# Second attention with float32 scores, each head in its own 32 rows of the array

## The chip, the cores and the metric

The kernel runs on one core of one Trainium2 chip. The metric is the device time of one execution in microseconds. The core's engines are named as in the profile: PE (TensorE, matmuls), PEld (its weight loads), DVE (VectorE), ACT (ScalarE), POOL (GpSimd) and SP, whose queue issues DMA transfers.

## What is computed

Eight sequences of 512 tokens with 128 features go through four residual steps. This case is about the third, a causal attention with 16 heads of 8 features and rotary position encoding:

```python
def _L1_attn_ref(x, W_qkv, W_out):        # x is layer-normed before
    qkv = jnp.einsum('bti,oi->bto', x, W_qkv)
    qkv = qkv.reshape(Bsz, Tlen, 3 * NUM_HEADS, HEAD_DIM).transpose(0, 2, 1, 3)
    q, k, v = jnp.split(qkv, 3, axis=1)
    q = _apply_rope(q, cos_sin); k = _apply_rope(k, cos_sin)
    scores = jnp.einsum('bhqd,bhkd->bhqk', q, k) / np.sqrt(HEAD_DIM).astype(np.float32)
    scores = jnp.where(causal[None, None], scores, -jnp.inf)
    attn = jax.nn.softmax(scores, axis=-1)
    o = jnp.einsum('bhqk,bhkd->bhqd', attn, v)
    o = o.transpose(0, 2, 1, 3).reshape(Bsz, Tlen, D_MODEL)
    return jnp.einsum('bti,oi->bto', o, W_out)

x = x + _L0_attn_ref(...)   # first attention: windowed, dilated and global
x = x + _L0_ffn_ref(...)    # mixture of experts
x = x + _L1_attn_ref(_layernorm(x, axis=-1), L1_attn_W_qkv, L1_attn_W_out)
x = x + _L1_ffn_ref(...)    # second mixture, two rounds
```

## The kernel before

The four steps run one after the other. Both attentions are one function, `attention` (line 35), called with `causal` false for the first (tiles named w...) and true for the second (tiles named c...). X, the residual, stays in SBUF.

The second attention has 32 slots: 8 sequences (b) by 4 groups (g) of 4 heads; slot n is b = n // 4, g = n % 4. One hand-written order of events, built by `slot` and `chain` and walked by every engine in `walk`, sets the order on each engine; semaphores tie the engines together. A slot has 8 units (i = 0 to 7). In unit i of slot n PE issues one matmul for maxima, the scores of the unit, a second matmul for maxima, and then the events put at i. The maxima belong to slots ahead: those of slot n + 1 in units 0 and 1, those of slot n + 2 in units 2 to 7.

- **Operands of the scores.** q and k are each split into three bfloat16 parts (`part1`, `left1`, `part2`, `left2`, on ACT and POOL, for the first sequence on DVE), written to DRAM (`parts_out`, line 787) and read back stacked into `QS` and `KS`, 72 rows of products a head (`stacks`, lines 798 and 802), with rows 96 to 98 for the maxima. `stacks` issues 6 DMAs a group, `parts_out` 6 a sequence.
- **Maxima** (`smax`, line 393): for each of 4 heads and 4 query blocks t one matmul, queries on the output partitions, (t + 1) x 128 keys as columns, into one of two buffers of the PSUM tile `SM`. DVE adds the mask and reduces it to one column of `NM` (line 622), after which the buffer is free. `maxima_parts` (lines 661 and 665) splits the 16 columns into three bfloat16 parts, PE turns them (`rows`, line 400), DVE copies the 12 rows (line 673) and SP writes them into `QS` with 3 DMAs (line 810).
- **Scores** (`scores`, line 417): unit i takes head i % 4 and two key blocks, 512 and 384 queries in units 0 to 3, 256 and 128 in units 4 to 7, into one of two buffers of `ST`; ACT takes the Exp (line 543), POOL zeroes above the diagonal (line 772).
- **Values**: `pv` (line 463) is float32 with 32 columns a head, so that four heads stand side by side in the array's columns, at unit 6 (first half) and unit 2 of the next slot (second half); `evac` (line 550) evicts it on ACT at unit 3, `sel` (line 472) turns the result at unit 5.
- **Once a sequence**: normalisation, `xT`, `proj` and `rot` (lines 369 and 375, q or k times cosine and a turned copy times sine, line 585, added in `join`), `values`, `vcopy`, `heads_T`, `out_proj`. `xT`, `values`, `rows`, `sel`, `heads_T` and `out_proj` share the PSUM bank `MI` in turn; `proj` and `rot` borrow halves of `ST` (`lend`).

POOL's queue also holds the gathers of the mixture's results into X (lines 711 and 719). SP's queue holds all the DMAs of the stage in program order.

Of the kernel before, what the change touches and what calls it, by code (L numbers as in the profile page):

```python
# [25 lines left out]
MR0 = 96  # L26

# [7 lines left out]
def attention(nc, X, const, w, scratch, causal, due=None):  # L35
# [19 lines left out]
    with nc.cleanup_on_exit(), ExitStack() as ctx:  # L55
# [6 lines left out]
        QS = sb("qs", [P, H, S], BF16)  # L62
        KS = sb("ks", [P, H, S], BF16)
        ML = sb("ml", [SPLIT, 2, 2 * HG, S], BF16)
# [9 lines left out]
        QK = sb("qk", [P, 2, S])  # L74
        QR = sb("qr", [P, 2, S])
        PT = sb("pt", [P, 2, SPLIT, S], BF16)
        TQ = sb("tq", [P, 2, S])
        M = sb("m", [P, HG, NT, NT * DIL])
        MD = sb("md", [P, HG, NT, NT * DIL])
        NM = sb("nm", [P, KINDS * HG, NT])  # L80
        NR = sb("nr", [P, KINDS * HG, NT])
        MT = sb("mt", [P, NT, MROWS], BF16)
        MR = sb("mr", [MROWS, S], BF16)
        OS = sb("os", [P, 2, S])
        JUNK = sb("junk", [P, 4, S], BF16) if causal else None
# [16 lines left out]
        s_pr = sem("pr")  # L102
# [23 lines left out]
        MRD = SPLIT if causal else 2 * SPLIT  # L126
        NNO = 2 if causal else 3
        NV = 1 if causal else 2
        NPT = 3 if causal else 2
# [7 lines left out]
        def second(g, at, put):  # L137

            for i in list(at):
                at[i] = [e for e in at[i] if not (e[1] == 1 and e[0] in ("part1", "left1", "part2", "left2", "parts_out"))]  # L140
            if g == 0:
                for t in range(NT):
                    put(2 * t + 1, "results", 2, t, 1)

        def slot(n):
# [13 lines left out]
            if causal:  # L159
                put(3, "evac", n - 1)  # L160
                put(CUT - 1, "maxima", n + 1)
                put(CUT + 1, "rows", n + 1)
                put(5, "sel", n - 1)
                if g == 0:
                    put(-1, "stacks", b, 3)
                    put(1, "part1", b + 1, 1)
                    put(3, "left1", b + 1, 1)
                    put(4, "vcopy", b, 2)
                    put(5, "part2", b + 1, 1)
                    put(6, "left2", b + 1, 1)  # L170
                    put(7, "parts_out", b + 1, 1)
# [7 lines left out]
                if g == 2:  # L179
# [3 lines left out]
                    put(4, "proj", b + 2, 0)  # L183
                    put(5, "rot", b + 2, 0)
                    put(7, "join", b + 2, 0)
                if g == 3:
                    put(0, "stacks", b + 1, 2)
                    put(1, "part1", b + 2, 0)
                    put(3, "left1", b + 2, 0)
                    put(4, "proj", b + 2, 1)  # L190
                    put(4, "vcopy", b + 1, 0)
                    put(4, "vcopy", b + 1, 1)
                    put(5, "part2", b + 2, 0)
                    put(5, "rot", b + 2, 1)
                    put(6, "left2", b + 2, 0)
                    put(7, "parts_out", b + 2, 0)
# [1897 lines left out]
```

## Time and profile before

| | us |
|---|---|
| median of 3 runs | 2036.46 (2025.91 to 2037.03) |
| the profiled execution | 2029.46 |
| its span, first to last instruction | 2027.8 |
| mean granted TensorE clock | 0.898 |
| PE busy in the span | 1630.1 (80%) |
| DVE busy | 1157.7 (57%) |
| ACT busy | 883.5 (44%) |
| POOL busy | 616.0 (30%) |

### The profile page before, as it was taken

To read this page: it belongs to the slowest core of one execution; us is meant where nothing else is said; L and a number is where in the kernel's file an instruction comes from. 1 tells how busy PE (TensorE), PEld (TensorE's weight loads), DVE (VectorE), ACT (ScalarE), POOL (GpSimd) and SP (SyncE) were. 2 spreads that over 40 slices of the span, in tenths; PEclk is the share of its full clock that TensorE was granted. 3 is DMA by queue.
4 is the path that set the end of the run, shared out by engine and by line. 5 is a ranking of instruction groups with operands and counts; after the bars stand their busy time and mean duration, and the time that the engine had idled before them with its cause. 6 is when DMAs were issued, how large, how long until landed. Compare 5 with 4: busy or idle time off the path is not lost. (4 is left out here: it accounts for less than half of the span.)

```text
span 2027.8 us, 35597 instructions
## 1 busy us (share of the span) xinstructions
PE 1630.1 (80%) x11387; PEld 888.1 (44%) x11489; DVE 1157.7 (57%) x3354; ACT 883.5 (44%) x1406; POOL 616.0 (30%) x879
## 2 busy tenths in 40 slices
PE   1899999999999999579899994468888888616683
PEld 1244444444444443355566663124444444514563
DVE  4756676656667664226333333468888877344584
ACT  1255555656565655431133331045555555402242
POOL 1001010101010100003522223376666533454467
PEclk8699999999999999679999997589999999557897
DMA  3110101111111100322011111233333220235442
GB/s 104 37 52 23 45 22 46 28 42 35 42 39 29 42 26 3 125 42 43 9 40 43 43 43 27 61 69 75 75 75 74 68 64 27 82 121 148 128 115 58
DMA packets 92786, 115.08 MB, mean 57 GB/s; under 512 B 13977, under 2 KB 76223, under 8 KB 92350
## 3 DMA queue, kind: packets, MB, share of 16 engines
q1 hardware_dynamic: 75710, 91.10, 16.5%
q0 software_dynamic: 16896, 21.69, 4.6%
q8 instruction: 99, 1.62, 0.3%
q14 instruction: 81, 0.66, 0.1%
HBM read 73.93 MB, written 39.34 MB: 56 GB/s over the span
## 5 line engine op out<-in xcount | busy, mean ns | idle before, releaser
L543 ACT ACTIVATE we<-wst 128x1024 f32<-128x1024 f32 x384 | 386.1, 1025 | 303.4 <-PE wst L430 158.8
L625 DVE TENSOR_REDUCE wm<-wsm 128x16 f32<-128x512 f32 x512 | 335.7, 685 | 259.5 <-PE wsm L393 255.6
L622 DVE CUSTOM_DVE_ANT_0 cjunk<-csm,const 128x128 bf16<-128x128 f32 (+3 forms) x512 | 232.5, 486 | 78.9 <-PE csm L393 70.3
L543 ACT ACTIVATE ce<-cst 128x896 f32<-128x896 f32 (+1 forms) x256 | 179.2, 704 | 186.0 <-PE cst L417 184.6
L393 PE MATMUL wsm<-wks,wqs 96*128 96x512 bf16 x512 | 191.3, 398 | 32.8 <-DMA wks<-qk_parts 20.2
L393 PE MATMUL csm<-cks,cqs 96*128 96x128 bf16 (+3 forms) x512 | 157.8, 315 | 69.1 <-DVE cnm L622 43.1
L772 POOL TENSOR_SCALAR_AFFINE_SELECT ce<-ce 128x256 f32<-128x256 f32 x256 | 125.3, 506 | 160.0 <-ACT ce L543 159.2
L434 PE MATMUL wst<-wqs,wks 128*128 128x512 bf16 x442 | 139.2, 385 | 9.5 <-issue 5.3
L1606 DVE TENSOR_TENSOR abhh<-absg,abup 128x512 f32<-128x512 f32 x72 | 49.5, 688 | 152.5 <-ACT absg L1585 152.5
L463 PE MATMUL woa<-we,wv 128*32 128x512 f32 x1024 | 132.0, 636 | 1.6 <-ACT we L543 1.6
L393 PEld LDWEIGHTS csm<-cks,cqs 96*128 96x128 bf16 x512 | 51.1, 100 | 182.6 <-DVE cnm L622 117.3
L1622 POOL DMA_INDIRECT abxb<-rows,asource x72 | 68.2, 947 | 162.3 <-DVE abys L1613 145.6
L417 PE MATMUL cst<-cqs,cks 128*128 128x384 bf16 (+3 forms) x480 | 106.6, 299 | 5.0 <-ACT ce L543 1.3
L422 PE MATMUL wst<-wml,const_b 3*128 3x512 bf16 x256 | 100.1, 391 | 9.3 <-ACT we L543 9.3
L430 PE MATMUL wst<-wqs,wks 96*128 96x128 bf16 x1024 | 105.9, 227 | 0.0
L1585 ACT ACTIVATE absg<-abup 128x512 f32<-128x512 f32 x72 | 43.0, 597 | 140.4 <-PE abup L1554 140.4
L393 PEld LDWEIGHTS wsm<-wks,wqs 96*128 96x128 bf16 x512 | 47.6, 98 | 122.5 <-DVE wm L625 61.0
L463 PE MATMUL coa<-ce,cv 128*32 128x512 f32 (+3 forms) x1024 | 92.3, 482 | 8.5 <-POOL ce L772 8.5
L430 PEld LDWEIGHTS wst<-wqs,wks 96*128 96x128 bf16 x1024 | 63.0, 108 | 60.1 <-issue 60.1
L761 POOL COPY wv<-wvs 128x128 f32<-128x128 f32 x32 | 9.3, 290 | 228.4 <-ACT wvs L503 200.2
L1554 PE MATMUL abup<-awg,abxt 128*128 x144 | 75.1, 604 | 2.3 <-ACT abxt L1591 2.3
L1574 PE MATMUL aby<-awd,abht 128*128 x576 | 76.2, 276 | 0.1
(318 smaller groups left out, 2987.7 us busy)
## 6 DMA issues: line engine op xcount, KB each, us to landing
wqs<-qk_parts SPq DMA_DIRECT2D x96, 96.0 KB
wks<-qk_parts SPq DMA_DIRECT2D x96, 96.0 KB
cqs<-qk_parts SPq DMA_DIRECT2D x96, 96.0 KB
cks<-qk_parts SPq DMA_DIRECT2D x96, 96.0 KB
b1r<-rows SPq DMA_DIRECT2D x40, 194.0 KB, 2.6
qk_parts<-wpt SPq DMA_DIRECT2D x48, 128.0 KB, 2.4
qk_parts<-cpt SPq DMA_DIRECT2D x48, 128.0 KB, 2.4
b0r<-rows SPq DMA_DIRECT2D x40, 130.0 KB, 2.5
```

The source lines that it names most:

```text
L393: pe.matmul(SM[:, j % 2, 0:keys], QS[0:MR0, h, t * P:(t + 1) * P], KS[0:MR0, h, 0:keys], start=True, stop=True, skip_group_check=True).the ...
L417: m = pe.matmul(st[:, at:at + width], KS[:, h, kb * P:(kb + 1) * P], QS[:, h, kb * P:S], start=True, stop=True, skip_group_check=True)
L422: pe.matmul(st[:, at:at + S], const["ones_b"][0:SPLIT, :], ML[:, g % 2, kind * HG + hs, :], start=True, stop=False, skip_group_check=True)
L430: m = pe.matmul(out, k, q, start=False, stop=(t == NT - 1), skip_group_check=True)
L434: m = pe.matmul(st[:, c * S:(c + 1) * S], KS[:, h, kb * P:(kb + 1) * P], QS[:, h, :], start=True, stop=True)
L463: m = pe.matmul(OA[VW * hs:VW * (hs + 1), S - width:S], V[:, kb, g * HG + hs, 0:VW], E[:, e_slot(g, HG * r + hs), at:at + width], start=(c ...
L543: act.activation(E[:, e_slot(g, i), 0:width], ST[:, (U * g + i) % 2, 0:width], ACT.Exp, scale=SCALE).then_inc(s_ex, 1)
L622: dve.tensor_tensor_reduce(JUNK[:, j % 4, 0:keys], SM[:, j % 2, 0:keys], const["mask_wide"][:, S - keys:S], 1.0, -3e38, ALU.add, ALU.max, ...
L625: dve.tensor_reduce(M[:, hs, t, :].rearrange("p (w f) -> p w f", f=DIL), SM[:, j % 2, :].rearrange("p (w i f) -> p w f i", w=NT, f=DIL), A ...
L772: pool.affine_select(e, e, [[0, 2], [1, P]], ALU.is_ge, 0.0, base=0, channel_multiplier=-1).then_inc(s_tri, 1)
L1554: m = pe.matmul(UP[:, i % 2, w, 0:F], XT[:, i % 2, :], weight[:, bass.ds(e * F, F)], start=True, stop=True)
L1574: m = pe.matmul(Y[:, j % 2, 0:D], HT[:, j % 2, c * P:(c + 1) * P], WD[:, bass.ds(e * HB * D + c * D, D)], start=(c == 0), stop=(c == HB - 1))
```

## The change

In the second attention only (`causal` true):

- q and k are not split. They stay float32 in the tile `QK`, now with two sequences' room, and 12 DMAs a group copy each head's 8 rows from there into the first 8 of the head's own 32 partitions, of `QM` (queries for the maxima), `KS` and `QS`. Nothing goes through DRAM; `part1`, `left1`, `part2`, `left2`, `parts_out` are gone.
- Maxima and scores are float32 matmuls over a head's 32 partitions (`lanes`). The maxima go by decreasing t, heads in the order 2, 3, 0, 1, so that the heads of a unit's maxima and scores all differ.
- A score unit is one key block and two heads, in the two banks of an `ST` buffer: 512 queries in units 0 and 1, 384 in 2 and 3, 256 in 4 and 5, 128 in 6 and 7.
- `maxima_parts` is gone: PE turns `NM` itself (float32), ACT and no longer DVE copies 4 rows, and SP writes each head's row by itself, 4 DMAs.
- `turned` takes the place of `proj` and `rot`: half of the tokens at a time, `qkv` and `rot` side by side in one bank (`MI` from the third sequence on, no longer `ST`), multiplied by a constant that holds cosines and sines side by side. It stands at other units, and `stacks` of group 0 at unit 0 in place of 3.

```diff
@@ slot
-                put(CUT - 1, "maxima", n + 1)
                 put(CUT + 1, "rows", n + 1)
                 put(5, "sel", n - 1)
                 if g == 0:
                     put(-1, "stacks", b, 3)
-                    put(1, "part1", b + 1, 1)
-                    put(3, "left1", b + 1, 1)
+                    put(1, "turned", b + 1, 1, 1)
+                    put(3, "join", b + 1, 1)
...
                 if g == 1:
                     put(0, "out_proj", b - 1)
-                    put(3, "stacks", b + 1, 0)
+                    put(0, "stacks", b + 1, 0)
...
-                    put(4, "proj", b + 2, 0)
-                    put(5, "rot", b + 2, 0)
-                    put(7, "join", b + 2, 0)
+                    put(6, "turned", b + 2, 0, 0)
                 if g == 3:
                     put(0, "stacks", b + 1, 2)
...
+                    put(0, "turned", b + 2, 0, 1)
+                    put(2, "join", b + 2, 0)
...
+                    put(6, "turned", b + 2, 1, 0)
@@ helpers
+        def lanes(hs):
+            return slice(LANES * hs, LANES * hs + LANES)
+        def unit(i):
+            kb, pair = divmod(i, 2)
+            return kb, 2 * pair, S - kb * P
+        def smax_of(j):
+            if causal:
+                return (2, 3, 0, 1)[j % HG], NT - 1 - j // HG
+            return divmod(j, NT)
@@ tensor
+            def turned(b, turn, side, half):
+                pe.wait_ge(s_xt, b + 1)
+                if b == 1:
+                    pe.wait_ge(s_rope, 2 * side + half + 1)
+                to = bank(b, "turned", 2 * side + half)
+                tok = xnT[:, half * S // 2:(half + 1) * S // 2]
+                pe.matmul(to[:, 0:S // 2], w["qkv"][:, side * D:(side + 1) * D], tok, start=True, stop=True, skip_group_check=True)
+                pe.matmul(to[:, S // 2:S], w["rot"][:, side * D:(side + 1) * D], tok, start=True, stop=True, skip_group_check=True
+                          ).then_inc(s_full, 1)
@@ smax
-                pe.matmul(SM[:, j % 2, 0:keys], QS[0:MR0, h, t * P:(t + 1) * P], KS[0:MR0, h, 0:keys], start=True,
-                          stop=True, skip_group_check=True).then_inc(s_sm, 1)
+                    pe.matmul(SM[:, j % 2, 0:keys], QM[lanes(hs), g, t * P:(t + 1) * P], KS[lanes(hs), g, 0:keys], start=True,
+                              stop=True, skip_group_check=True).then_inc(s_sm, 1)
@@ rows
+                    pe.wait_ge(s_mx, SMU * (n + 1))
+                    for t in range(NT):
+                        m = pe.transpose(MI[0:HG, t * P:(t + 1) * P], NM[:, n % 2, t, :], const["ident"])
@@ scores
-                    for kb, at, width in cols(i // HG):
-                        m = pe.matmul(st[:, at:at + width], KS[:, h, kb * P:(kb + 1) * P], QS[:, h, kb * P:S],
-                                      start=True, stop=True, skip_group_check=True)
+                    kb, first, width = unit(i)
+                    for c in range(2):
+                        m = pe.matmul(st[:, c * S:c * S + width], KS[lanes(first + c), g, kb * P:(kb + 1) * P],
+                                      QS[lanes(first + c), g, kb * P:S], start=True, stop=True, skip_group_check=True)
@@ sync, stacks and rows
+                if causal:
+                    sp.wait_ge(s_pt[0], b + 1)
+                    sp.wait_ge(s_pt[1], b + 1)
+                    for to, side in ((QM, 0), (KS, 1), (QS, 0)):
+                        got = QK[g * HG * DH:(g + 1) * HG * DH, b % 2, side, :]
+                        for hs in range(HG):
+                            sp.dma_start(to[LANES * hs:LANES * hs + DH, g, :], got[hs * DH:(hs + 1) * DH, :]
+                                         ).then_inc(s_rd[g], 16)
+                    return
...
+                if causal:
+                    for hs in range(HG):
+                        at = LANES * hs + MAXROW
+                        sp.dma_start(QS[at:at + 1, g, :], MR[hs:hs + 1, :]).then_inc(s_ml, 16)
+                    return
```

## Rows read from the trace of the kernel before

**Rows 1.** The page, its first line: the span.

```profile
span 2027.8 us, 35597 instructions
```

**Rows 2.** The eviction of `oa` into `os`: count, ns, first and last start.

```profile
L550 ACT ACTIVATE cos<-coa x32: 592/592/597, 1350.1 to 1731.6; 128x512 f32<-128x512 f32 x32
```

**Rows 3.** Timeline of ACT: start us, duration us, instruction [idle before].

```profile
1479.54 0.59 ACT L550 ACTIVATE cos<-coa 128x512 f32<-128x512 f32 x1
...
1491.91 0.59 ACT L550 ACTIVATE cos<-coa 128x512 f32<-128x512 f32 x1
...
1504.03 0.59 ACT L550 ACTIVATE cos<-coa 128x512 f32<-128x512 f32 x1
...
1518.15 0.60 ACT L550 ACTIVATE cos<-coa 128x512 f32<-128x512 f32 x1
```

**Rows 4.** Busy time by window: PE, PEld, DVE, ACT, POOL, PEclk, DMA, GB/s.

```profile
1401.00:1452.00 51.00, 44.97 (x332) 21.89 (x334) 41.55 (x172) 27.40 (x44) 34.64 (x52) 0.97 0.32 74
```

**Rows 5.** Waits between 1350 and 1700 us: waiter, releaser, total, times, longest.

```profile
PEld csm L393 <- DVE cnm L622: 95.8, 182, 1.8
```

**Rows 6.** Groups by shape, 1323 to 1735 us: count, busy us, mean ns.

```profile
L622 DVE CUSTOM_DVE_ANT_0 cjunk<-csm,const 128x512 bf16<-128x512 f32 x122 | 84.0, 689 | 2.3 <-PE csm L393 1.2
L622 DVE CUSTOM_DVE_ANT_0 cjunk<-csm,const 128x384 bf16<-128x384 f32 x122 | 67.7, 555 | 48.0 <-PE csm L393 44.5
L622 DVE CUSTOM_DVE_ANT_0 cjunk<-csm,const 128x256 bf16<-128x256 f32 x121 | 50.7, 419 | 6.6 <-PE csm L393 6.5
L622 DVE CUSTOM_DVE_ANT_0 cjunk<-csm,const 128x128 bf16<-128x128 f32 x121 | 34.0, 281 | 7.0 <-PE csm L393 3.2
```

**Rows 7.** Timeline of PE in the second attention.

```profile
1479.82 1.08 PE L369 MATMUL cst<-cxnT,w1t 128*128 128x512 f32 x2
...
1481.28 0.98 PE L472 MATMUL cmi<-const,cos 128*128 128x36 f32 x8
1482.09 1.11 PE L375 MATMUL cst<-cxnT,w1r 128*128 128x512 f32 x2
...
1483.46 1.71 PE L463 MATMUL coa<-ce,cv 128*32 128x512 f32 x16
...
1486.10 0.23 PE L393 MATMUL csm<-cks,cqs 96*128 96x128 bf16 x1 [0.28 <-DVE cnm L622]
...
1488.92 0.86 PE L463 MATMUL coa<-ce,cv 128*32 128x256 f32 x16
```

**Rows 8.** Timeline of DVE beside it.

```profile
1480.93 0.69 DVE L585 TENSOR_TENSOR ctq<-cst,const 128x512 f32<-128x512 f32 x1 [0.42 <-PE cst L369]
...
1485.96 0.08 DVE L622 DVE_READ_ACCUMULATOR2_ANT cnm<- 128x1 f32 x1
```

**Rows 9.** Timeline of PE in the first attention.

```profile
501.80 0.37 PE L422 MATMUL wst<-wml,const_b 3*128 3x512 bf16 x1 [0.33 <-ACT we L543]
502.10 0.40 PE L430 MATMUL wst<-wqs,wks 96*128 96x128 bf16 x4
...
503.00 0.59 PE L393 MATMUL wsm<-wks,wqs 96*128 96x512 bf16 x2
```

**Rows 10.** The page's costliest groups: the Exp of 1024 columns.

```profile
L543 ACT ACTIVATE we<-wst 128x1024 f32<-128x1024 f32 x384 | 386.1, 1025 | 303.4 <-PE wst L430 158.8
```

**Rows 11.** Timeline of DVE around the split of the maxima.

```profile
1500.98 0.20 DVE L661 CAST cmt<-cnm 128x16 bf16<-128x16 f32 x1
...
1502.11 0.29 DVE L622 CUSTOM_DVE_ANT_0 cjunk<-csm,const 128x128 bf16<-128x128 f32 x1
```

**Rows 12.** Timeline of SP's queue at the stage's start.

```profile
1280.45 3.81 SPq L787 DMA_DIRECT2D qk_parts<-cpt  x6
...
1305.09 1.94 SPq L810 DMA_DIRECT2D cqs<-cmr  x3
```

**Rows 13.** Timeline of PE there.

```profile
1293.55 0.50 PE L393 MATMUL csm<-cks,cqs 96*128 96x128 bf16 x2 [15.89 <-DMA cks<-qk_parts]
...
1323.83 0.52 PE L417 MATMUL cst<-cqs,cks 128*128 128x384 bf16 x1 [0.22 <-issue]
```

More of the change, by code:

```diff
@@ L26 @@
 MR0 = 96
+LANES = P // HG
+MAXROW = DH
 SCALE = float(DH) ** -0.5
@@ L101, in attention @@
         s_pj = sem("pj")
-        s_pr = sem("pr")
         s_vs = sem("vs")
@@ L139, in second @@
             for i in list(at):
-                at[i] = [e for e in at[i] if not (e[1] == 1 and e[0] in ("part1", "left1", "part2", "left2", "parts_out"))]
+                at[i] = [e for e in at[i] if not (e[1] == 1 and e[0] in ("turned", "join"))]
             if g == 0:
@@ L273, in attention @@
         order += [("smax", 0, j) for j in range(SMU)]
-        order += [("maxima", 0), ("rows", 0)]
+        order += [("rows", 0)] if causal else [("maxima", 0), ("rows", 0)]
         if causal:
@@ L284, in bank @@
         def bank(b, name, which):
-            if b and (name == "values" or not causal):
+            if b >= 2 or (b and (name == "values" or not causal)):
                 return MI[:, :]
@@ L316, in walk @@
                     eng.wait_ge(s_init, 2 * NV)
-                    eng.wait_ge(s_ones, 2)
+                    eng.wait_ge(s_ones, NONES)
                 if e[0] not in handlers:
                     continue
-                own = e[0] in ("proj", "rot", "values") and e[1] == 0
+                own = (e[0] in ("proj", "values") and e[1] == 0) or (e[0] == "turned" and e[1] < 2)
                 if e[0] in BANK and eng is nc.tensor and turn and not own:
@@ L486, in out_proj @@
                 m.then_inc(s_full, 1)
-            walk(pe, dict(xT=xT, proj=proj, rot=rot, values=values, smax=smax, rows=rows, scores=scores, pv=pv,
+            walk(pe, dict(xT=xT, proj=proj, turned=turned, values=values, smax=smax, rows=rows, scores=scores, pv=pv,
                           sel=sel, heads_T=heads_T, out_proj=out_proj))
@@ L541, in scores, with rows @@
                     act.wait_ge(s_pv, R * n + r - 1)
-                width = (sum(c[2] for c in cols(r)) if causal else 2 * S)
-                act.activation(E[:, e_slot(g, i), 0:width], ST[:, (U * g + i) % 2, 0:width], ACT.Exp, scale=SCALE
-                               ).then_inc(s_ex, 1)
+                if causal:
+                    width = unit(i)[2]
+                    act.activation(E[:, i, 0:2 * width].rearrange("p (c q) -> p c q", c=2),
+                                   ST[:, i % 2, :].rearrange("p (c q) -> p c q", c=2)[:, :, 0:width], ACT.Exp, scale=SCALE
+                                   ).then_inc(s_ex, 1)
+                else:
+                    act.activation(E[:, e_slot(g, i), :], ST[:, (U * g + i) % 2, :], ACT.Exp, scale=SCALE).then_inc(s_ex, 1)
+            def rows(n, g, b, turn):
+                if not causal:
+                    return
+                act.wait_ge(s_full, turn + 1)
+                if n:
+                    act.wait_ge(s_ml, 16 * MRD * n)
+                act.activation(MR[:, :], MI[0:HG, :], ACT.Copy).then_inc(s_mr, 1)
             def evac(n, g, b, turn):
@@ L553, in heads_T @@
                 lay(turn, MI[:, :], OT[:, :], s_ot, from_phases)
-            walk(act, dict(xT=xT, proj=proj, part1=part1, part2=part2, values=values, scores=scores, evac=evac, heads_T=heads_T))
+            walk(act, dict(xT=xT, proj=proj, part1=part1, part2=part2, values=values, rows=rows, scores=scores, evac=evac, heads_T=heads_T))
         @block.vector
```

209 lines of the change are left out of this document (98 added, 111 removed).

## The prediction

> **What bounds the kernel now.** I read the page first for the span, 2027.8 us, which with 1.7 us around it is the profiled execution's 2029.5 us [rows 1]; the sum below is made against that. It lies 7.0 us under the median of the three runs, 2036.5, and inside their 11 us spread. Only the second attention is changed. It has 32 slots (8 sequences by 4 groups of 4 heads), and each ends its product with the values in one eviction of the tile `oa`: the rows of that tile give the first at 1350.1 and the last at 1731.6 us [rows 2]. Four neighbouring evictions stand 12.37, 12.12 and 14.12 us apart [rows 3]; with a fourth distance of 12.37 a sequence takes 51.0 us, 12.8 us a slot (the long one is the slot with the projections' rest and `heads_T`). Of the 381.5 us from first to last, 28 distances at 12.8 take 358 and the last three, which have few maxima left to prepare, 23 us. In one whole sequence of 51 us PE is busy 45.0 us and DVE 41.6 us at a granted clock of 0.97 [rows 4]: no single engine is full, two are nearly so. What ends their waits is each other: PE's loads for the maxima stood 95.8 us waiting for DVE [rows 5], because the score tile for the maxima (`sm`) has two buffers, a matmul may start only when DVE has reduced the buffer two steps back, and everything behind that wait in PE's queue stands too. So I price the change by this ring and by what interrupts it on PE.
>
> **The change, part by part.**
> *Maxima.* Sixteen matmuls a slot stay, with 512, 384, 256 and 128 keys four times each, now float32 on 32 rows. DVE's work stays: with the trailing accumulator read a reduction holds its buffer about its mean plus 0.01 us, 0.70, 0.56, 0.43 and 0.29 us [rows 6]. PE's part is read from the projection, the only float32 matmul with 128 stationary columns here: one matmul is two records, both together take 1.08 us for 512 columns [rows 7]. The products with the values show the rate: 16 records, four column groups of 512 and 384 columns in two passes, last 1.71 us [rows 7]; less some 0.2 us of lead and drain that is 1792 columns in 1.5 us, 0.83 ns a column and pass, with the four groups at once. So a float32 matmul of w columns streams 1.67 ns times w (0.85, 0.64, 0.43, 0.21 us) and is read by DVE 0.23 us later than that. The hand-over PE to DVE is 0.03 us (1480.90 to 1480.93), DVE to PE 0.06 us (1486.04 to 1486.10) [rows 7, 8]. One turn of a buffer is then 1.08 + 0.03 + 0.70 + 0.06 = 1.87 us at 512 keys, 1.52 at 384, 1.18 at 256, 0.82 at 128. Two buffers turn together, so a unit (two maxima, one pair of scores) takes at least one turn. Before, a head of four widths took 2.0 us, 8.0 us a slot.
> *Scores.* Each unit is now two heads on one key block, two matmuls in different rows and banks, 512 queries in units 0 and 1, then 384, 256, 128. I take the four matmuls of a unit, which use four different row groups, to run side by side, as the four column groups do [rows 7]; no row shows it for row groups. Weight loads follow one another at 0.10 us: eight pairs of load and matmul of `mi` start within 0.81 us [rows 7]. In units 0 and 1 scores rule: 0.3 us of loads, 1.08 us, an Exp of 1024 columns at 1.03 us [rows 10] and 0.1 us of hand-overs, 2.5 us for two buffers, 1.25 a unit. Units 2 to 7 go by the turns: 2 x (1.87 + 1.52 + 1.18) = 9.1.
> *What interrupts the row groups.* PV, `sel`, the transposes and projections use other shapes. The trace prices the change of shape in the first attention: a 3-row matmul of 512 columns keeps the next from starting for 0.30 us, while a second 512-column record adds only 0.59 - 0.37 = 0.22 [rows 9], so about 0.09 us each way. A unit with an interruption is longer than its turn: both its maxima must first have streamed (seven loads, 0.7 us, and the stream), then comes the interruption and 0.2 us of switching. Unit 2 with PV of 256 and 128 columns: 1.55 + 0.64 + 0.2 = 2.4. Unit 3 with four float32 transposes of the maxima (128 columns, one pass, 0.43 us): 2.2. Unit 4: 1.5. Unit 5 with `sel`: 1.34 + 0.81 + 0.2 = 2.35. Unit 6 with PV of 512 and 384: 1.13 + 1.49 + 0.2 = 2.8. Unit 7: 1.2. With 2.5 for units 0 and 1 that is 14.95 us.
> *Work once a sequence.* Four `turned` (as many float32 columns as `proj` and `rot`, 0.85 + 0.2 each), two sets of transposes (0.6 each), `values` and `out_proj` (about 1.0 each, as `sel`): 7.4 us, 1.85 a slot. They too now cost a switch each way, and in the slots that have them `turned` waits for the bank `mi`. Sum: 16.8 us a slot.
> The same bookkeeping, without hiding, gives 13.2 to 14.3 us for the slot before (8.0 of maxima, 2.5 of PV, 1.1 of `rows` and `sel`, 1.6 once a sequence, and up to 1.1 for the split), where 12.8 is measured: it overstates by 0.4 to 1.5. So I take 16.8 less half the larger error, 16.1 us, with 15.3 and 16.8 as ends: **+3.3 us a slot** (2.5 to 4.0).
> *Removed.* The split of the maxima in three is four small DVE operations, 1.13 us from the first to the next reduction [rows 11], and DVE's copy of the row (0.41) moves to ACT, where two of the copies for the parts go away. DVE is no longer what sets the ring, so this relief, and that on POOL, is already in the sum, not beside it.
> *Stacks.* SP issues 12 DMAs a group for 6, and 4 rows for 3. At 0.65 us each [rows 12] a slot's 16 cost 10.4 us of SP's 16.1; the rows, behind the 12, go out 8 us into the slot and land well before the next slot's first score. Cover is gone when a slot is under about 12 us. At the start the way through DRAM goes: before, its first write was issued at 1280.45 [rows 12] and the first maximum ran at 1293.55 [rows 13]. Now 12 DMAs from 1278.3, 7.8 us, and about 2 us to land give 1288: 5 us won. But 16 + 12 float32 maxima before the first score (1323.83 [rows 13]) take 2.6 x 4 + 9.1 = 19.5 us at full clock against 16, more at the low clock there, and the split saves 2. I take 0, between -5 and +5.
> *The end.* The last three distances keep scores and PV; I put 2 to 3 us on each, +7.
> Sum: 2029.5 + 28 x 3.3 + 7 = 2129, **2130 us**.
>
> **Rivals.** *Row groups share less than fully.* If maxima and scores take turns and only the pair overlaps, a slot streams 8.5 + 4.3 + 2.1 + 0.8 + 0.4, with 1.85 and 0.8 of switches 18.8 us: +6.0, 2205 us. If every stream is 1.3 times as long, the six turns gain 1.15 and units 0 and 1 0.3 us a slot: 2170. For it: nothing in the trace shows row groups; against: the column groups do run at once [rows 7]. The Trainium skill ("TensorE: Matmul & The Clock Gate", Measured speedup vs the span model) measured 3.07 times for four row groups of 512 columns, not 4; as an estimate by that page, 4 / 3.07, the streams would be 1.3 times as long, the 2170 case. No run here shows it yet.
> *None overlap, or the clock falls.* 8.5 + 8.5 of maxima and scores make the slot 23.1 us, +10.3: about 2340. If the chip counts 32 busy rows as idling and grants 1.2 GHz, all streams double, about the same. Against the latter: PV's 32-column float32 does not lower it now (0.97 [rows 4]).
> *Not slower.* If a 32-row float32 matmul streamed as fast as bfloat16 now (0.22 us for 512 columns [rows 9]), the ring would again be DVE's: 12.8 less about 0.8 for split and copy, plus 0.5 for switches, and 9 us at the start, 2010 us. It decides once the six turns' 3.8 us of streams fall under about 0.5 to 1. Against: the rate in rows 7 is that of the type, not of the number of columns used.
>
> **How the numbers follow.** Forecast 0.70, its own range 2090 to 2160 (15.3 and 16.8 us a slot, and 10 to 15 us for the start, the end and DVE's other work falling into a turn); partial sharing 0.10; no sharing or low clock 0.12; not slower 0.08, of which 0.05 beyond 1%. About 1% is what a measurement of this kernel can tell from no change. The range reaches over forecast and partial sharing: 2075 to 2215. Slower by over 1% 0.92, within 0.03, faster 0.05.
>
> **What would show it.** Right: evictions of `oa` 15.3 to 16.8 us apart; DVE's busy time in the stage lower while its waits for the maxima's matmuls grow; score pairs whose two matmuls start within 0.3 us of each other; fewer 3.4 us stretches at low clock. Wrong: pairs that start one stream apart (no sharing), a clock near 0.5, a first score much earlier or later than 1324 us, or slots waiting for `cqs<-cmr`, where SP would be the bound. The largest doubt is the 2.5 to 4.0 us a slot, which is how much DVE's reductions still hide behind PV and `sel`.

## The result, and the profile after

The changed kernel takes 2167.7 us (median of 4 runs, 2164.1 to 2169.3), the kernel before 2035.7 us beside it: a ratio of 1.066, with a 95% interval of 1.062 to 1.069, so 132 us slower. The forecast was 2130 us, range 2075 to 2215, slower by over 1% at 0.92.

The page of the changed kernel, its first line and three of its costliest groups (out<-in, count, busy us, mean ns, idle us before, and what ended it), to be read beside [rows 1, 2, 6]:

```profile
span 2164.7 us, 37748 instructions
...
L635 DVE CUSTOM_DVE_ANT_0 cjunk<-csm,const 128x256 bf16<-128x256 f32 (+3 forms) x512 | 237.9, 489 | 188.1 <-PE csm L394 185.7
L394 PE MATMUL csm<-cks,cqm 32*128 32x512 f32 (+3 forms) x1024 | 301.3, 521 | 34.5 <-ACT ce L553 11.6
...
L424 PE MATMUL cst<-cqs,cks 32*128 32x512 f32 (+3 forms) x1024 | 210.1, 506 | 1.4 <-ACT ce L553 1.4
```

The eviction of `oa`, which ends each slot, answers to [rows 2]:

```profile
L571 ACT ACTIVATE cos<-coa x32: 592/592/597, 1363.6 to 1869.0; 128x512 f32<-128x512 f32 x32
```

DVE's reductions cost what they did (237.9 us in 512), but DVE now idles 188 us before them, waiting for the matmuls of the maxima. The waits (waiter, releaser, total, times, longest) say it again. Before, between 1350 and 1700 us, DVE's wait beside that of [rows 5]:

```profile
DVE cjunk L622 <- PE csm L393: 40.8, 63, 3.2
```

and after, between 1380 and 1780 us:

```profile
DVE cjunk L635 <- PE csm L394: 115.5, 179, 3.2
PEld csm L394 <- DVE cnm L635: 68.1, 142, 1.4
```

DVE waits for PE 115.5 us of 400 where it was 40.8 of 350, and PE's loads wait less for DVE (68.1 us of 400 for 95.8 of 350): the ring has turned round, and it is mostly PE that is late.

The 28 slots from the first eviction to the 29th, busy time by engine, PEclk, DMA share and GB/s. First before:

```profile
1350.10:1708.30 358.20, 310.83 (x2312) 152.15 (x2340) 286.94 (x1196) 190.42 (x297) 205.51 (x339) 0.97 0.28 69
```

and after:

```profile
1363.60:1835.00 471.40, 451.44 (x3285) 214.82 (x3284) 257.36 (x1056) 193.16 (x301) 178.84 (x313) 0.91 0.11 18
```

PE is busy 451 of 471 us where it was busy 311 of 358, DVE works 30 us less. The granted clock is lower although PE idles less: a mean of 0.91 is about 18% of the time at 1.2 GHz, 83 us by the clock's record, against 24 us (7%) before.

Where the 136.9 us between the two spans went, by the same landmarks in both traces:

| stretch | before | after | difference |
|---|---|---|---|
| up to the mixture's end (code not changed) | 1241.3 | 1252.0 | +10.7 |
| from there to the first eviction | 108.8 | 111.6 | +2.8 |
| 28 slots | 358.3 (12.80 each) | 471.5 (16.84 each) | +113.2 |
| last three slots | 23.3 | 34.0 | +10.7 |
| the rest (code not changed) | 296.2 | 295.7 | -0.5 |

The first row is variation of the runs and not the change: in the kernels tried below that share this part, the same landmark (the start of the mixture's last `abys`) lies between 1239.4 and 1251.5 us (1251.5 in `x_bf16`). Most of it is the clock's: inside the first attention, whose code is the same, 51 us are at the lower level after and 34 before, and it ends 7.4 us later. So the change is worth some 126 us in these two executions, nine tenths of it in the slots.

What is inside 4 us a slot shows when the slots are looked at one by one. These are seven neighbouring slots of the changed kernel (window, length, busy times, PEclk, DMA, GB/s). Slots 1 and 5, 2 and 6, 3 and 7 hold the same kind of work, since a sequence has four:

```profile
1380.78:1398.57 17.79, 17.19 (x119) 7.52 (x119) 9.42 (x37) 6.52 (x12) 6.97 (x11) 0.90 0.11 18
1398.57:1417.33 18.76, 18.21 (x115) 8.56 (x116) 9.40 (x37) 6.40 (x12) 7.48 (x13) 0.82 0.13 20
1417.33:1432.59 15.26, 14.89 (x126) 7.42 (x124) 8.61 (x36) 7.17 (x13) 7.88 (x12) 1.00 0.13 21
1432.59:1451.40 18.81, 17.37 (x123) 8.54 (x123) 9.89 (x47) 7.60 (x14) 8.02 (x13) 0.82 0.14 22
1451.40:1467.52 16.12, 15.52 (x118) 7.31 (x119) 9.39 (x37) 6.50 (x12) 6.97 (x11) 1.00 0.12 20
1467.52:1483.07 15.55, 15.00 (x115) 7.36 (x116) 9.41 (x37) 6.40 (x11) 7.55 (x13) 1.00 0.16 25
1483.07:1499.97 16.90, 16.52 (x126) 7.65 (x123) 8.62 (x36) 7.17 (x12) 7.88 (x12) 0.90 0.12 19
```

The slot at 1398.57 takes 18.76 us at a mean clock of 0.82, its twin at 1467.52 takes 15.55 at 1.00: 3.2 us more for 6.8 us at the lower clock, 0.47 us for each. An engine at half speed loses half of the time it spends there, 0.5 us for each, so nearly nothing of PE's delay hides. At that price the low clock costs 39 us in the 28 slots after (83 x 0.47). Before, every slot that has low clock lacks a twin without it; I take the same price there, 11 us (24 x 0.47), as an estimate: DVE is nearer to being the bound there, and it may be less. So of the +113 us some 28 are the clock's (39 at most), and 85 are the work's, 3.0 us a slot. Without the low clock a slot takes 15.4 us after (471.5 less 39, by 28).

Last, a slot at full clock, PE's timeline (start us, duration us, instruction), units 4 to 7, answering to [rows 7]:

```profile
1417.57 0.58 PE L394 MATMUL csm<-cks,cqm 32*128 32x384 f32 x1
1417.58 0.70 PE L424 MATMUL cst<-cqs,cks 32*128 32x256 f32 x4
1417.90 0.91 PE L394 MATMUL csm<-cks,cqm 32*128 32x384 f32 x3
1419.14 0.58 PE L394 MATMUL csm<-cks,cqm 32*128 32x384 f32 x1 [0.33 <-DVE cnm L635]
...
1420.45 1.08 PE L486 MATMUL cmi<-const,cos 128*128 128x36 f32 x8
1421.46 0.48 PE L394 MATMUL csm<-cks,cqm 32*128 32x256 f32 x1
1421.47 0.38 PE L424 MATMUL cst<-cqs,cks 32*128 32x128 f32 x2
1421.48 0.48 PE L394 MATMUL csm<-cks,cqm 32*128 32x256 f32 x1
1421.68 0.28 PE L424 MATMUL cst<-cqs,cks 32*128 32x128 f32 x2
1421.78 0.39 PE L394 MATMUL csm<-cks,cqm 32*128 32x256 f32 x2
1422.11 1.71 PE L470 MATMUL coa<-ce,cv 128*32 128x512 f32 x16
1423.75 0.48 PE L394 MATMUL csm<-cks,cqm 32*128 32x256 f32 x1
```

From 1421.46 on, the first records of two maxima and two scores, in four row groups, start within 0.02 us of each other, and the second records 0.2 to 0.3 us later: the row groups do work side by side. How long they take together shows in unit 1 of this slot, with two scores of 512 columns beside two maxima of 128:

```profile
1427.22 0.37 PE L394 MATMUL csm<-cks,cqm 32*128 32x128 f32 x1
1427.23 0.70 PE L424 MATMUL cst<-cqs,cks 32*128 32x512 f32 x2
...
1427.76 0.59 PE L424 MATMUL cst<-cqs,cks 32*128 32x512 f32 x2
```

Both scores are done 1.12 us after they started, where the projection alone took 1.08 [rows 7].

### The profile page after: what moved, and what is told of

Same layout as the page of the kernel before. It is cut to its first block and busy times, and to the rows that moved or that the text cites. A ratio compares the mean times of both kernels' runs of the same rounds, so it can differ in the third digit from the quotient of the medians.

```text
span 2164.7 us, 37748 instructions
## 1 busy us (share of the span) xinstructions
PE 1819.3 (84%) x12507; PEld 976.7 (45%) x12577; DVE 1115.9 (52%) x3191; ACT 883.7 (41%) x1406; POOL 587.0 (27%) x851
## 5 line engine op out<-in xcount | busy, mean ns | idle before, releaser
L635 DVE CUSTOM_DVE_ANT_0 cjunk<-csm,const 128x256 bf16<-128x256 f32 (+3 forms) x512 | 237.9, 489 | 188.1 <-PE csm L394 185.7
L394 PE MATMUL csm<-cks,cqm 32*128 32x512 f32 (+3 forms) x1024 | 301.3, 521 | 34.5 <-ACT ce L553 11.6
L553 ACT ACTIVATE ce<-cst 128x1024 f32<-128x1024 f32 (+3 forms) x256 | 178.0, 703 | 323.7 <-PE cst L424 321.3
L424 PE MATMUL cst<-cqs,cks 32*128 32x512 f32 (+3 forms) x1024 | 210.1, 506 | 1.4 <-ACT ce L553 1.4
L394 PEld LDWEIGHTS csm<-cks,cqm 32*128 32x128 f32 x1024 | 134.7, 200 | 163.6 <-DVE cnm L635 105.2
L792 POOL TENSOR_SCALAR_AFFINE_SELECT ce<-ce 128x256 f32<-128x256 f32 x256 | 119.9, 471 | 322.4 <-ACT ce L553 321.2
L477 PE MATMUL woa<-we,wv 128*32 128x512 f32 x1024 | 136.8, 656 | 1.6 <-ACT we L557 1.6
L470 PE MATMUL coa<-ce,cv 128*32 128x512 f32 (+3 forms) x1024 | 111.0, 562 | 1.0 <-POOL ce L792 1.0
L424 PEld LDWEIGHTS cst<-cqs,cks 32*128 32x128 f32 x1024 | 82.5, 196 | 6.9 <-ACT ce L553 3.7
```

Of the source, the lines that this page charges most:

```text
L394: pe.matmul(SM[:, j % 2, 0:keys], QM[lanes(hs), g, t * P:(t + 1) * P], KS[lanes(hs), g, 0:keys], start=True, stop=True, skip_group_check=T ...
L424: m = pe.matmul(st[:, c * S:c * S + width], KS[lanes(first + c), g, kb * P:(kb + 1) * P], QS[lanes(first + c), g, kb * P:S], start=True, s ...
L470: m = pe.matmul(OA[VW * hs:VW * (hs + 1), kb * P:S], V[:, kb, g * HG + hs, 0:VW], E[:, 2 * kb + hs // 2, hs % 2 * width:(hs % 2 + 1) * width],
L477: m = pe.matmul(OA[VW * hs:VW * (hs + 1), :], V[:, kb, g * HG + hs, 0:VW], E[:, e_slot(g, HG * r + hs), c * S:(c + 1) * S], start=False, s ...
L553: act.activation(E[:, i, 0:2 * width].rearrange("p (c q) -> p c q", c=2), ST[:, i % 2, :].rearrange("p (c q) -> p c q", c=2)[:, :, 0:width ...
L635: dve.tensor_tensor_reduce(JUNK[:, j % 4, 0:keys], SM[:, j % 2, 0:keys], const["mask_wide"][:, S - keys:S], 1.0, -3e38, ALU.add, ALU.max, ...
```

## The experiments

Two theories stood against each other for the 132 us. **Streams**: a float32 matmul takes two passes of 0.43 us for 512 columns [rows 7] where a bfloat16 one takes a single one of 0.22 [rows 9], the ring of the maxima becomes PE's, and sharing between row groups takes only part of that back. **Clock**: matmuls on 32 rows bring stretches at 1.2 GHz, whatever their type. All runs give the ratio to the kernel before, run on the same chip beside them. Differences in microseconds between runs on different chips are good to a few microseconds only.

### The type alone: `x_bf16`

The changed kernel with its stacks and the row of maxima in bfloat16 and nothing else different. (The scores are then single bfloat16 products.)

```diff
-            QM = sb("qm", [P, NG, S])
-            QS = sb("qs", [P, NG, S])
-            KS = sb("ks", [P, NG, S])
-            QK = sb("qk", [P, 2, 2, S])
+            QM = sb("qm", [P, NG, S], BF16)
+            QS = sb("qs", [P, NG, S], BF16)
+            KS = sb("ks", [P, NG, S], BF16)
+            QK = sb("qk", [P, 2, 2, S], BF16)
...
-            MR = sb("mr", [HG, S])
+            MR = sb("mr", [HG, S], BF16)
```

> The changed kernel with the tiles QK, QM, KS, QS and MR in bfloat16: same order, same DMAs, same row groups, one record a matmul in place of two (the scores lose precision, nothing is left out). Theory of the streams: the slot is long because 32-row float32 matmuls stream four times as many cycles; the ring then turns at DVE's pace (about 2.0 us a head) and the slot falls from 16.8 to 12.2 to 13.2 us, the time to 2030 to 2065 us. Rival, the order and the transfers (12 + 4 DMAs a slot, turned through mi, the switches of shape): the slot stays at 15 us or more, the time above 2110. Rival, 32 busy rows lower the clock whatever the type: the granted clock of the stage stays at or under 0.91; by the streams it goes back to about 0.95 or more.

2044.4 us, ratio 1.0055 (1.0029 to 1.0082): all but 11 us of the loss is gone, so the type carries most of it. But the kernel before has the DVE work of the split, 72 rows of products and a way through DRAM on top, and is still not slower. The 28 slots of this run say why (columns as before):

```profile
1343.40:1722.00 378.60, 324.51 (x2388) 148.02 (x2387) 248.48 (x1054) 186.33 (x301) 178.86 (x315) 0.81 0.10 15
```

DVE is 38 us less busy than before, and the clock is 0.81: 144 of 379 us (38%) at the lower level. The slots without any of it (six of the 28) take 11.8 us on average, all together 13.5, a little over the 12.2 to 13.2 of the streams. Both theories have hit; each holds for a part.

### The number of rows: `x_bf16_rows`

`x_bf16` with `KS` holding a copy for each head in which the other heads' 96 rows are zero, so that every maximum and score uses all 128 rows and gives the same numbers: rows that hold zeros are in use here.

```diff
-            KS = sb("ks", [P, NG, S], BF16)
+            KS = sb("ks", [P, H, S], BF16)
...
-                    pe.matmul(SM[:, j % 2, 0:keys], QM[lanes(hs), g, t * P:(t + 1) * P], KS[lanes(hs), g, 0:keys], start=True,
+                    pe.matmul(SM[:, j % 2, 0:keys], QM[:, g, t * P:(t + 1) * P], KS[:, h, 0:keys], start=True,
```

> The bfloat16 form of the changed kernel (x_bf16), with all 128 rows of the array in use in every matmul of maxima and scores: KS holds each head by itself, its own 32 rows filled and the other 96 zero, and the moving or stationary side takes the four heads' rows at once. Same products, same columns, same DMAs; nothing runs side by side any more, but the streams are short. Theory: the matmuls on 32 rows bring the low clock. Then the low clock goes from 38% of the stage to under 10%, and although the matmuls stand in a row the time falls by 10 to 35 us against x_bf16 (2044), to 2010 to 2035. Rival, short waits of PE bring it (rows in use do not count): the low share stays above 25% and the time rises by 5 to 40 us.

2002.7 us, ratio 0.9873 (0.9834 to 0.9912): 42 us faster than `x_bf16` (37 by the two ratios), with row groups that can share nothing. That is more than the 10 to 35 us expected. Its 28 slots:

```profile
1332.40:1675.00 342.60, 299.22 (x2392) 161.09 (x2391) 248.40 (x1056) 186.16 (x301) 178.84 (x315) 0.99 0.11 17
```

PEclk is 0.99, 4 us of 343 at the lower level. The scores' group on this run's page also shows the one wait that the prediction had put under 12 us a slot, for the row of maxima on SP's queue:

```profile
L424 PE MATMUL cst<-cqs,cks 128*128 128x256 bf16 (+3 forms) x512 | 113.2, 304 | 9.5 <-DMA cqs<-cmr 7.6
```

### Sharing in float32: `x_f32_rows` and `x_clash`

`x_f32_rows` is the same edit on the changed kernel, in float32. It takes the sharing away altogether.

```diff
-            KS = sb("ks", [P, NG, S])
+            KS = sb("ks", [P, H, S])
...
-                        m = pe.matmul(st[:, c * S:c * S + width], KS[lanes(first + c), g, kb * P:(kb + 1) * P],
-                                      QS[lanes(first + c), g, kb * P:S], start=True, stop=True, skip_group_check=True)
+                        m = pe.matmul(st[:, c * S:c * S + width], KS[:, g * HG + first + c, kb * P:(kb + 1) * P],
+                                      QS[:, g, kb * P:S], start=True, stop=True, skip_group_check=True)
```

> The same edit on the changed kernel itself, float32: 128 rows in use in every matmul of maxima and scores, so that the four matmuls of a unit stream one after the other. It prices the sharing of the array. By the prediction's sum for no overlap (8.5 + 8.5 us of streams a slot) the slot is 22 to 23.5 us and the time 2300 to 2350 us, at a granted clock of nearly 1. If the row groups gave little, the time is near 2168 or below it.

2334.8 us, ratio 1.1501 (1.1470 to 1.1532). The 28 slots:

```profile
1357.00:1997.00 640.00, 640.00 (x3286) 391.09 (x3284) 266.12 (x1055) 199.38 (x301) 178.44 (x313) 1.00 0.08 13
```

22.86 us a slot, PE busy all of it at full clock. That is the prediction's sum for no overlap (23.1 us, 2340). Against 15.3 to 16.1 us for full-clock slots of the changed kernel, sharing is worth 7 us a slot. Two matmuls of 512 columns, which took 1.12 us side by side, stand one after the other here, four records 0.43 us apart:

```profile
1506.20 1.88 PE L424 MATMUL cst<-cqs,cks 128*128 128x512 f32 x4
```

`x_clash` takes part of it: the maxima go through the heads as 0, 1, 2, 3, so that in every unit both maxima need the very row groups of the unit's two scores.

```diff
-                return (2, 3, 0, 1)[j % HG], NT - 1 - j // HG
+                return j % HG, NT - 1 - j // HG
```

> The changed kernel with one edit: the maxima take the heads in the order 0, 1, 2, 3, so that in every unit the two maxima use the same two row groups as the pair of scores. If disjoint row groups run side by side and this carries the slot, each unit's second maximum waits for a score's stream (0.2 to 0.4 us in most units): the slot grows by 1 to 2 us and the time by 30 to 60 us. If row groups share little anyway, or the order of heads does not matter because the ring is longer than the streams, the time stays within 10 us of 2168.

2240.0 us, ratio 1.0992 (1.0951 to 1.1033): 72 us above the changed kernel, more than the 30 to 60 expected. The clock is what was left out of the expectation. In the 28 slots

```profile
1357.00:1908.00 551.00, 538.48 (x3282) 324.67 (x3282) 262.65 (x1054) 194.31 (x300) 178.96 (x313) 0.82 0.10 16
```

201 of 551 us are at the lower level, 118 us more than in the changed kernel; at 0.47 us each they cost 55 us (twin slots of this run, 17.02 us at full clock and 20.19 with 6.8 us of low clock, give the same price). The 28 slots are 80 us longer, which leaves 25 for the lost sharing. Fewer row groups at once, and more low clock: this called for a run in which there is never more than one.

### One row group, never shared: `x_bf16_lane0` and `x_f32_lane0`

Every head's stack is held in rows 0 to 31, so that matmuls follow one another as in the runs with 128 rows, but on 32 rows each.

```diff
-            KS = sb("ks", [P, NG, S], BF16)
+            KS = sb("ks", [LANES, H, S], BF16)
...
-                    pe.matmul(SM[:, j % 2, 0:keys], QM[lanes(hs), g, t * P:(t + 1) * P], KS[lanes(hs), g, 0:keys], start=True,
+                    pe.matmul(SM[:, j % 2, 0:keys], QM[:, h, t * P:(t + 1) * P], KS[:, h, 0:keys], start=True,
...
-                            sp.dma_start(to[LANES * hs:LANES * hs + DH, g, :], got[hs * DH:(hs + 1) * DH, :]
+                            sp.dma_start(to[0:DH, g * HG + hs, :], got[hs * DH:(hs + 1) * DH, :]
```

> The changed kernel with its stacks and row of maxima in bfloat16, and with every head held in rows 0 to 31 instead of its own 32 rows, so that the heads' score matmuls follow one another and never run side by side. (The scores are then single bfloat16 products.) TensorE is occupied as long as in the run with all 128 rows (slots of 12.24 us there, 1% of the stage at the low clock, 2003 us), but each score matmul uses 32 rows. If the number of rows in use brings the low clock: at least 25% of the 28 slots' time at the lower clock, slots of 13.5 us or more, 2035 to 2070 us. If it is the way in which four row groups work at once (gaps and turns between them) that brings it, and a serial order keeps it up: under 10% at the lower clock, slots of about 12.2 us, 1995 to 2012 us. I give the first 0.6.

2180.1 us, ratio 1.0675 (1.0643 to 1.0707). The 28 slots:

```profile
1342.00:1840.00 498.00, 475.79 (x2387) 212.70 (x2385) 255.96 (x1054) 195.33 (x300) 178.72 (x313) 0.63 0.07 12
```

> The changed kernel in float32 as it is, with every head held in rows 0 to 31, so that nothing is shared between row groups. The run with all 128 rows in float32 took 22.86 us a slot, none of it at the lower clock, and 2335 us. If the number of rows in use brings the low clock: at least 15% of the slots' time at the lower clock, slots of 25 us or more, 2390 us or more. If a serial order keeps the clock up whatever the rows: 22.9 us a slot, 2325 to 2345 us. In both cases at least 60% longer slots than the 15.3 us that full-clock slots of the changed kernel take, since the sharing is gone.

2952.6 us, ratio 1.4471 (1.4423 to 1.4520). The 28 slots:

```profile
1390.00:2564.00 1174.00, 1174.00 (x3286) 614.97 (x3284) 270.00 (x1055) 200.10 (x302) 178.20 (x313) 0.56 0.05 7
```

In both the clock falls further than I had put as a lower bound: 369 of 499 us and 1044 of 1174 us at 1.2 GHz. The time of `x_bf16_lane0` lies 110 us above the range that I had given for this case. The float32 pair settles it. The same matmuls, as many, in the same order, with PE busy the whole time in both: on 128 rows the clock is 1.00 and a slot 22.86 us, on 32 rows 0.56 and 41.91 us. It is not gaps that lower the clock here, nor the type, nor the number of matmuls; it is that the matmuls of the maxima and the scores use 32 of the 128 rows. (A slot that is at 1.2 GHz throughout takes 46.04 us on 32 rows, and the same slot at full clock 22.83 on 128: twice as long.) The Trainium skill ("TensorE: Matmul & The Clock Gate", Why this matters for your kernels) ties a fall of the clock to idle gaps of the engine; this run has none and falls, so here the measurement decides.

In order of the rows at work at a time, the low share of the 28 slots is then:

| stacks | rows at a time | float32 | bfloat16 |
|---|---|---|---|
| all 128 rows | 128 | 0% (`x_f32_rows`) | 1% (`x_bf16_rows`) |
| row groups, four heads a unit | up to 128 | 18% (the change) | 38% (`x_bf16`) |
| row groups, two heads a unit | up to 64 | 37% (`x_clash`) | - |
| rows 0 to 31 only | 32 | 89% (`x_f32_lane0`) | 74% (`x_bf16_lane0`) |

### Maxima in bfloat16, scores in float32: `x_hyb`, `x_hyb_rows`

A version that keeps the change's float32 scores but takes the maxima from bfloat16 copies of q and k (a maximum is only subtracted, and cancels in the normalisation). `x_hyb` has 16 stack DMAs a group for 12; `x_hyb_rows` puts its maxima on 128 rows as above.

```diff
+            KM = sb("km", [P, NG, S], BF16)
+            QB = sb("qb", [P, 2, 2, S], BF16)
...
-                    pe.matmul(SM[:, j % 2, 0:keys], QM[lanes(hs), g, t * P:(t + 1) * P], KS[lanes(hs), g, 0:keys], start=True,
+                    pe.matmul(SM[:, j % 2, 0:keys], QM[lanes(hs), g, t * P:(t + 1) * P], KM[lanes(hs), g, 0:keys], start=True,
```

> The changed kernel with the maxima alone in bfloat16 (tiles QM and KM from a bfloat16 copy of QK, made by a second addition; 16 stack DMAs a group in place of 12); the scores stay float32. A maximum that is a little off cancels in the softmax. Theory of the ring: it is the maxima's stream, 0.85 us for 512 keys in each turn of a buffer, that makes the slot long; units 2 to 7 go back to DVE's pace and the slot falls by 2.5 to 3.5 us, the time to 2070 to 2100 us, unless SP's 20 DMAs of 0.66 us (13.2 us) become the bound. If the scores' streams matter as much, it stays above 2120.

> The kernel with bfloat16 maxima and float32 scores (x_hyb), with the maxima alone over 128 rows (KM zero outside each head's rows); the scores keep their 32-row pairs. If rows in use decide the clock, the low share falls from 35% to under 15% and the time from 2120 to 2075 to 2100 us, although maxima and scores no longer run side by side. If the maxima's waits decide, it stays within 10 us of 2120 or rises.

2120.3 us (ratio 1.0432, 1.0397 to 1.0466) and 2139.0 us (1.0549, 1.0516 to 1.0582). The slots between the same two times, `x_hyb` first:

```profile
1346.00:1785.00 439.00, 398.20 (x2842) 198.10 (x2840) 252.43 (x1055) 188.10 (x301) 192.54 (x326) 0.82 0.12 20
1346.00:1785.00 439.00, 424.95 (x2838) 200.78 (x2837) 256.90 (x1056) 192.52 (x301) 192.23 (x325) 0.95 0.12 20
```

Both miss the time of their first theory, and both times fall to the rival's side: 2120.3 lies just above 2120, and `x_hyb_rows` rises. In `x_hyb` 155 of 439 us are at the lower level, of which the expectation knew nothing; 155 - 83 = 72 us more than in the change, at 0.47 us each 34, would put it at 2086. In `x_hyb_rows` that share falls to 10%, as the number of rows in use says, but its full-clock slots take 14.8 us on average where those of `x_hyb` take 13.5: a matmul over all rows shares with none. The profiled execution of `x_hyb_rows` (2114.7 us) is 24 us faster than its median, so I read no more out of it.

### Only the split taken away: `v_one`, `v_both`

What the change gives back to DVE, alone: the kernel before, with the maxima of the second attention written as one bfloat16 part in place of three (`v_one`), and those of the first too (`v_both`). The scores keep their three parts.

```diff
-    MROWS = KINDS * HG * SPLIT
+    MPARTS = 1 if causal else SPLIT
+    MROWS = KINDS * HG * MPARTS
...
+                if causal:
+                    dve.tensor_copy(part[:, 0], NM[:, :, :]).then_inc(s_ms, 1)
+                    return
```

> The kernel before with the maxima of the second attention rounded to one bfloat16 part in place of three (one cast, no subtractions, one row DMA; the same rounded value stands in numerator and denominator, so it cancels). It prices the split alone. If DVE set the ring before, 0.9 us of DVE a slot come free and most of the slots get 0.4 to 0.9 us shorter: 13 to 28 us, 2008 to 2023 us. If the split lay wholly beside PV on PE, nothing changes: within 5 us of 2036.

> The kernel before with maxima rounded to one bfloat16 part in both attentions (v_one has it in the second alone, 2016 us). In the first attention PE, not DVE, is nearly full, and the split lies beside its work: 0 to 8 us further, 2008 to 2018 us. If DVE's split delayed the row there, more.

2016.4 us (ratio 0.9921, 0.9897 to 0.9945) and 1997.5 us (0.9833, 0.9804 to 0.9861). A slot of the second attention takes 12.31 us for 12.80. The first attention ends at 806.6 us in `v_both` and at 824.4 in `v_one`: 17.8 us for 32 slots, where I had expected at most 8. It would be more at equal clock, since `v_both` happened to have 41 us at the lower level there and `v_one` 20. Four slots of the same kinds at full clock, `v_one` and then `v_both`:

```profile
299.89:393.34 93.45, 87.10 (x747) 40.37 (x756) 60.75 (x126) 55.26 (x63) 7.91 (x14) 1.00 0.13 37
107.40:197.46 90.06, 86.44 (x756) 40.99 (x756) 57.72 (x114) 54.85 (x63) 7.88 (x14) 1.00 0.12 37
```

That is 0.85 us a slot, 27 us for 32. That DVE's chain between two rings of maxima is in the path there too is the likely cause, but the edit also leaves out four of the six DMAs for the row, and the two were not taken apart.

### The two gains together: `v_rows_both`

`x_bf16_rows` with the one-part maxima of `v_both` in the first attention.

```diff
-    MROWS = KINDS * HG * SPLIT
+    MROWS = KINDS * HG
...
-                for i in range(SPLIT):
+                for i in range(1):
```

> The form with stacks in bfloat16 over all 128 rows in the second attention (2003 us; its scores are single bfloat16 products), with the first attention's maxima taken from one bfloat16 part as well. The first attention gave 18.8 us when the same edit was made on the kernel before (2016 to 1998 us). If the two gains add up: 1978 to 1992 us. If the first attention's gain came from how the low clock fell there and not from matmuls left out: 1995 to 2003 us.

1999.0 us, ratio 0.9779 (0.9746 to 0.9812), not the 1978 to 1992 expected. The kernel before was slower on this chip (2042.7 us), so by the ratios it gains about 1% on `x_bf16_rows` (0.9873), as the edit should; in microseconds it gains 4. The first attention did become as short as in `v_both` (it ends at 803.6 us). The second gave some back: its 28 slots take 12.71 us for 12.24, of which 24 us instead of 4 are at the lower clock (some 9 us). The rest is not settled. By its ratio it is the fastest of all, with single bfloat16 scores, but its interval overlaps that of `v_both` (0.9804 to 0.9861). Of those that keep the precision of the scores, `v_both` is the fastest, and faster than both kernels.

## Why the prediction was right, and where it was not

The side, the range and the mechanism of the slots hold; the clock, which the sum put at nothing, does not. The time is 38 us above the forecast and 8 above the forecast's own range. About 11 of the 38 lie ahead of the second attention, in code that is not changed. The stated range reached up to 2215 for the sake of partial sharing, which did not happen; that the low clock filled the room is luck.

**The ring.** Right. The ring of the maxima is now PE's: [rows 5] gave 95.8 us of waits of PE's loads for DVE, now they wait 68.1, and DVE waits 115.5 us for the matmuls for 40.8. The price of the streams, 1.67 ns a column from [rows 7], is confirmed by the run without sharing: 0.43 us a record of 512 columns, and 22.86 us a slot against the 23.1 of the sum. (By the forecast's own way of adding up, +10.3 us a slot is 2325 us, not the 2340 that the prediction wrote.)

**Sharing between row groups.** Right, though no row showed it: the four starts within 0.02 us above, and 7 us a slot in `x_f32_rows`. The rival "share less than fully" had 2170 in it, which is nearly the time measured. It is right by number and not by mechanism: streams 1.3 times as long would make the slots at full clock 17.5 us (16.1 and the rival's 1.45), and these take 15.3 to 16.1 us; two scores of 512 columns beside two maxima took 1.12 us for the 1.08 of one alone. The Trainium skill's 3.07 for four row groups ("TensorE: Matmul & The Clock Gate", Measured speedup vs the span model), from which that case was drawn, stays neither shown nor refuted: no run here times four 512-column matmuls by themselves.

**The slot, +3.3 us.** Measured at +4.0, and made of two errors that partly cancel: the work costs +3.0, less than forecast, and the low clock +1.0, which the forecast had at nothing. The bookkeeping of units was right where nothing interrupts and too high where something does. In the full-clock slot from 1417.57 on (units 7 and 0 predicted with the 0.6 of `heads_T`, the 1.0 of `out_proj` and 0.2 of switching each):

| unit | predicted | measured |
|---|---|---|
| 4 | 1.5 | 1.57 |
| 5, `sel` | 2.35 | 2.32 |
| 6, PV | 2.8 | 2.29 |
| 7, `heads_T` | 2.0 | 1.23 |
| 0, `out_proj` | 2.45 | 2.24 |
| 1 | 1.25 | 1.15 |
| 2, PV | 2.4 | 2.27 |
| 3, `rows` | 2.2 | 1.91 |

The step that was sized wrong is "both its maxima must first have streamed (seven loads, 0.7 us, and the stream)": after `sel` both buffers were free, the second maximum started 0.02 us after the first, and the loads of different row groups did not queue. PV began 0.65 us after the unit, not 1.13. Taking off half of the larger error (0.7 us), as the prediction did, covered about half of this: the sum had 16.8 us, the forecast 16.1, and without low clock a slot takes 15.4.

**The clock.** Wrong, and the step that failed. "Fewer 3.4 us stretches at low clock" was named as a sign of being right; there are 18 in place of 7, seven of them twice as long, and 83 us for 24. The argument was that PE would idle less (it does, 20 us in the 28 slots for 47), and that the products with the values, 32 columns in float32, do not lower the clock. They use all 128 rows of the array and 32 of its columns; the scores use 32 rows. The rival "the clock falls" named the mechanism with 2340 for all of the stage; here it is 18% of the 28 slots, and 28 us. That sharing between row groups keeps it there is what `x_clash` (37%) and `x_f32_lane0` (89%) point to.

**The start, 0.** +2.8 measured. SP's timeline there, beside [rows 12]:

```profile
1286.85 2.71 SPq L819 DMA_DIRECT2D cqm<-cqk  x4
1289.61 2.63 SPq L819 DMA_DIRECT2D cks<-cqk  x4
1292.27 2.63 SPq L819 DMA_DIRECT2D cqs<-cqk  x4
```

and PE's, beside [rows 13]:

```profile
1296.26 2.08 PE L394 MATMUL csm<-cks,cqm 32*128 32x512 f32 x4 [10.47 <-DMA cqs<-cqk]
```

Twelve DMAs at 0.66 us took 8.0 us (7.8 predicted), the last landed 1.3 us later, and the first maximum came 44.3 us after the mixture's end for 52.2: 8 us won, 5 predicted. From the first maximum to the first score, 39.6 us for 30.3: 9 lost, where the prediction balanced 3.5 us of streams against 2 of split at full clock. Of the 39.6 us 33 are at the lower clock, of the 30.3 before 23. Gain and loss were both larger than thought and nearly cancel. The last 1.4 us lie between the first score and the first eviction.

**The end, +7.** +10.7 measured. The last three slots, before and after:

```profile
1708.40:1731.60 23.20, 19.01 (x171) 8.75 (x173) 8.88 (x38) 13.76 (x24) 8.72 (x22) 1.00 0.01 2
1835.00:1869.00 34.00, 30.77 (x228) 13.70 (x228) 7.24 (x32) 15.01 (x27) 8.77 (x22) 0.85 0.01 2
```

The clock, 1.00 before, is 0.85 after: 10 us at the lower level, some 5 us at 0.47 each. So the work is about +6, near the forecast, and what it lacked is again the clock.

**SP.** Right: 16 DMAs a slot at 0.66 us are 10.5 of 16.8 us, and nothing waits for them; `x_bf16_rows`, with 12.2 us a slot, shows the bound that was put at 12.

In one sum: 28 x 3.0 for the work, 28 for the clock in the slots, 3 and 11 at the ends (5 of the 11 the clock's), 126 us, beside the 92, 0, 0 and 7 forecast.

## What to carry to other kernels

Price a float32 matmul by its own two records, and let row groups share only where the matmuls of one unit all sit in different ones: here sharing is worth 7 us of a 22.9 us slot, and an order of heads that clashes loses some 70 us. Before putting small heads on 32 rows each, see what the granted clock does: in bfloat16, zero rows that fill the array up to 128 added no columns to stream and brought some 40 us; in float32, where sharing is worth more than the clock, they cost some 170. And look for the chain of small operations that feeds a ring: taking the three-part split out of the maxima, which cancel anyway, gave 33 us by itself, where the new layout, which takes the split out too, lost 132.

## What the chip did that I had not expected

- Matmuls on 32 rows go with the lower clock even when PE never idles: 0.56 on average over 1174 us, against 1.00 with the same matmuls on 128 rows. The kernel before, with 96 and 128 rows, has 0.97 in its 28 slots; other numbers of rows were not tried by themselves.
- Float32 and bfloat16 matmuls in four row groups start within 0.02 us of each other. In float32 on 32 rows the second record of 512 columns starts 0.53 us after the first (1427.23 to 1427.76), on 128 rows 0.43.
- Low clock costs this kernel 0.47 us for each us, out of the 0.5 that half speed can cost: although DVE, ACT and the DMAs share the ring with it, nearly all of PE's delay reaches the time.
- Copies of 8 rows from SBUF to SBUF issue at 0.66 us each on SP, and the last of twelve landed about 1.3 us after its issue.
